# Two attention layers and two feed-forward layers on one core: the weight loads moved behind the first three quads of Q and K, and K of the second projection split on all 128 rows

## The reference, cut to what matters

```python
x = x + _L0_attn_ref(_layernorm(x), L0_attn_Wqvk, L0_attn_Wo)
x = x + _L0_ffn_ref(_layernorm(x), L0_ffn_router_w, ...)
x = x + _L1_attn_ref(_layernorm(x), L1_attn_w_q, L1_attn_w_k, ...)
x = x + _L1_ffn_ref(_layernorm(x), L1_ffn_W1, ...)
```

```python
q = q * rf
k = k * rf
qkt = jnp.einsum('brkqa,bkca->brkqc', q5, k) / scale
attn = jax.nn.softmax(qkt, axis=-1)
```

## Time and profile before

| | before |
|---|---|
| median of 3 runs | 1875.59 us (1871.88 to 1877.41) |
| profiled execution | 1856.86 us |
| its span | 1855.0 us |
| mean granted TensorE clock | 0.943 of full speed |
| TensorE matmul busy | 1708.5 us (92%) |
| TensorE weight load busy | 723.3 us (39%) |
| VectorE busy | 1372.3 us (74%) |
| ScalarE busy | 1143.6 us (62%) |
| GpSimd busy | 308.6 us (17%) |
| DMA moved | 93.73 MB, mean 51 GB/s |
| chain that ended last | PE 73%, DVE 14%, ACT 4%, issue 4%, POOL 3%, DMA 3% |

### The profile page before, as it was taken

The page is one execution under the profiler, slowest core; times in us unless marked ns, Lnnn a source line. Parts: engine busy times, 40 slices in busy tenths (PEclk is TensorE's granted clock), DMA queues, the critical chain, the costliest instruction groups (busy, mean ns, idle before and its releaser), DMA issues.

```text
span 1855.0 us, 30812 instructions
## 1 busy us (share of the span) xinstructions
PE 1708.5 (92%) x10574; PEld 723.3 (39%) x10574; DVE 1372.3 (74%) x2373; ACT 1143.6 (62%) x2396; POOL 308.6 (17%) x407
## 2 busy tenths in 40 slices
PE   6599999999999899998789999999999999999876
PEld 3244444444443366655312232232222222322455
DVE  7678888788887155464897888888888888882486
ACT  4156666756664543333406777777777777777776
POOL 5000000002231237363500000000000000000265
PEclk9589999999998899999658999999999999998998
DMA  9555454423400012222411111111111111000000
GB/s 258 137 118 127 131 141 118 49 31 56 58 22 14 26 35 71 68 67 60 119 33 14 18 18 18 18 18 18 18 18 18 18 18 18 1 2 1 1 23 24
DMA packets 97577, 93.73 MB, mean 51 GB/s; under 512 B 47214, under 2 KB 75507, under 8 KB 95376
## 3 DMA queue, kind: packets, MB, share of 16 engines
q1 hardware_dynamic: 87360, 53.70, 16.7%
q0 software_dynamic: 9920, 37.87, 5.8%
q10 hardware_dynamic: 144, 0.20, 0.1%
HBM read 48.03 MB, written 40.86 MB: 48 GB/s over the span
## 4 chain that ended last, share of the span: by engine, by line
PE 73%; DVE 14%; ACT 4%; issue 4%; POOL 3%; DMA 3%; SPq 0%; POOLq 0%; DVEq 0%; ACTq 0%
PE ps L877 20%; PE ps L861 18%; PE ps L828 17%; DVE rowmax L1513 7%; PE ps L1038 2%; PE ps L1058 2%; PE ps L1030 2%; PE ps L1048 2%; PE ps L893 2%; PE ps L831 1%; PE ps L864 1%; ACT probs L1251 1%; DMA V<-v 1%; PE ps L1015 1%; DVE K L1857 1%
## 5 line engine op out<-in xcount | busy, mean ns | idle before, releaser
L1513 DVE TENSOR_REDUCE rowmax<-ps 128x1 f32<-128x1024 f32 (+7 forms) x1024 | 977.1, 987 | 220.4 <-PE ps L828 120.9
L1251 ACT ACTIVATE probs<-ps 128x512 f32<-128x512 f32 (+3 forms) x1280 | 604.0, 537 | 268.8 <-PE ps L864 128.7
L828 PE MATMUL ps<-K,Q 72*128 72x512 bf16 (+3 forms) x1792 | 535.6, 377 | 40.2 <-DVE rowmax L1513 18.1
L861 PE MATMUL ps<-Q,K 75*128 75x512 bf16 (+3 forms) x1792 | 559.7, 364 | 11.0 <-ACT probs L1251 6.4
L861 PEld LDWEIGHTS ps<-Q,K 75*128 75x128 bf16 x1792 | 168.5, 98 | 373.4 <-ACT probs L1251 128.6
L877 PE MATMUL ps<-probs,V 128*9 128x512 f32 (+3 forms) x2560 | 289.9, 543 | 0.0
L828 PEld LDWEIGHTS ps<-K,Q 72*128 72x128 bf16 x1792 | 159.4, 99 | 280.3 <-DVE rowmax L1513 88.4
L1251 ACT ACTIVATE wu<-ps 128x512 f32<-128x512 f32 x256 | 142.0, 608 | 44.7 <-PE ps L861 43.9
L1251 ACT ACTIVATE wg<-ps 128x512 f32<-128x512 f32 x256 | 143.7, 601 | 29.0 <-PE ps L861 27.1
L616 POOL TENSOR_SCALAR rtmp<-mv 128x4 f32<-128x4 f32 x8 | 1.9, 233 | 805.6 <-DVE mv L1429 805.6
L831 PE MATMUL ps<-causal,identb 128*128 128x128 bf16 x512 | 117.0, 230 | 0.0
(11 more groups left out here) (239 smaller groups left out, 1667.8 us busy)
## 6 DMA issues: line engine op xcount, KB each, us to landing
dispatch<-wg POOLq DMA_DIRECT2D x16, 1170.0 KB, 7.9
Q<-q_parts SPq DMA_DIRECT2D x288, 64.0 KB
K<-k_parts SPq DMA_DIRECT2D x144, 64.0 KB
Q<-dispatch SPq DMA_DIRECT2D x78, 65.0 KB, 1.8
q_parts<-Q POOLq DMA_DIRECT2D x12, 384.0 KB, 4.0
probs<-returned SPq DMA_DIRECT2D x8, 512.0 KB, 3.9
V<-v SPq DMA_DIRECT2D x16, 144.0 KB
K<-k_parts SPq DMA_DIRECT2D x144, 16.0 KB
```

The lines of the kernel that those rows point to most:

```text
L828: last = pe.matmul(buf[:, c:e], Q[0:CROSS, slot, j, i * P:(i + 1) * P], K[0:CROSS, slot, kj, c:e], start=True, stop=not diag)
L861: last = pe.matmul(ps[:, bank, c:HALF], K[0:KROWS, q, kj, t * P:(t + 1) * P], Q[0:KROWS, q, j, h * HALF + c:(h + 1) * HALF], start=True, s ...
L1251: act.activation(prob(l, 4 * m + j)[:, c:HALF], ps[:, B_BANKS[(4 * m + j) % 3], c:HALF], ACT.Exp, scale=SCALE).then_inc(sl["exp_done"], 1)
L1513: dve.tensor_reduce(rowmax[:, par, 8 * j + i:8 * j + i + 1], score_a(i % 2)[:, 0:hd.keys(i)], AX, ALU.max).then_inc(sl["max_done"], 1)
```

## The change

Three things are changed. First, SP issues the twenty weight loads no longer at its start, but in layer 0 after the rows of group 0 and quad 2; quad 2 itself goes behind the rows of group 0 there. TensorE's wait for all weights moves from the start of attention 0 to the first "WO" step. Second, the K of projection 1 is computed in four chunks of 128 tokens, chunk j on the partitions 32j to 32j+31: four matmuls of 128 columns accumulate in one bank, each with a window of `wk_wide` as its weights, a tile of zeros with `wk1` in its middle. So the steps of splitting K run on 128 partitions and 128 columns. The rope factors for it are loaded in that layout (`ropeK`, four transfers by SP in the expert stage), VectorE writes `wk_wide` there too, and POOL writes K's parts with three transfers a block. Both new tiles lie in `compared`, which is free by then. Third, projection 1 uses four buffers for the parts as projection 0 does, so that the second attention's first output waits for all parts to be written. `PARTS` holds what each write adds to the ring's semaphores: 32, and 64 in projection 1.

```diff
+KVD = KV * HD
+PARTS = (32, 16 + 16 * SPL)
...
-            if l == 0 and u % 4 >= 2:
+            if u % 4 >= 2:
                 return parts_ahead[:, u % 2, :, :, :]
...
+        ropeK = compared[:, 0, 0:2 * P].rearrange("p (h n) -> p h n", h=2)
+        wk_wide = compared[:, 1, 0:2 * P - KVD]
...
-            s[l]["parts_written"] = [sem(f"parts_written{l}_{k}") for k in range((4, 2)[l])]
+            s[l]["parts_written"] = [sem(f"parts_written{l}_{k}") for k in range(4)]
...
                 sp.sem_inc(semaphore, 1)
-            for dst, source in weights:
-                sp.dma_start(dst, source).then_inc(w_in, 16)
             sp.sem_inc(ff["y_out"], FC)
...
                 sp.wait_ge(sl["v_taken"], NG + AT_ONE)
                 for written in sl["parts_written"]:
-                    sp.wait_ge(written, 32 * NG // len(sl["parts_written"]))
-                load(0, 2)
+                    sp.wait_ge(written, PARTS[l] * NG // len(sl["parts_written"]))
+                if l == 1:
+                    load(0, 2)
                 negmax_rows(0, 0)
+                if l == 0:
+                    load(0, 2)
+                    for dst, source in weights:
+                        sp.dma_start(dst, source).then_inc(w_in, 16)
...
+                            if g and t == TS:
+                                for j in range(GT):
+                                    sp.dma_start(ropeK[j * KVD:(j + 1) * KVD, :, :],
+                                                 rope[0:KVD, :].rearrange("i (h j n) -> j i h n", h=2, j=GT)[j])\
+                                        .then_inc(ropeK_in, 16)
...
-                        pool.dma_start(k_parts[l][:, :, bass.ts(u, GW)].rearrange("c p n -> p c n"),
-                                       parts_of(l, u)[0:rows_k, 1, :, :]).then_inc(written, 16)
+                        if l == 0:
+                            pool.dma_start(k_parts[l][:, :, bass.ts(u, GW)].rearrange("c p n -> p c n"),
+                                           parts_of(l, u)[:, 1, :, :]).then_inc(written, 16)
+                        else:
+                            for c in range(SPL):
+                                pool.dma_start(k_parts[l][c, :, bass.ts(u, GW)].rearrange("p (j n) -> j p n", j=GT),
+                                               parts_of(l, u)[:, 1, c, 0:P]).then_inc(written, 16)
...
-                    pe.matmul(ps[0:rk, bank + 2, :], wk, h[:, :], start=True, stop=True).then_inc(sl["k_out"], 1)
+                    if l == 0:
+                        pe.matmul(ps[:, bank + 2, :], wk, h[:, :], start=True, stop=True).then_inc(sl["k_out"], 1)
+                    else:
+                        for j in range(GT):
+                            last = pe.matmul(ps[:, bank + 2, 0:P], wk_wide[:, (GT - 1 - j) * KVD:(GT - 1 - j) * KVD + P],
+                                             h[:, j * P:(j + 1) * P], start=j == 0, stop=j == GT - 1)
+                        last.then_inc(sl["k_out"], 1)
...
                     if kind == "WO":
+                        if u == 0:
+                            pe.wait_ge(w_in, 16 * len(weights))
...
             pe.wait_ge(consts, 5)
-            pe.wait_ge(w_in, 16 * len(weights))
             attention(0)
...
-                rows = (P, P if l == 0 else KV * HD)
+                cols = (GW, GW if l == 0 else P)
...
-                            dve.tensor_tensor(qk32[0:rows[n], n, :], src[n], ropeT[0:rows[n], half * GW:(half + 1) * GW],
-                                              ALU.mult).then_inc(sl["qk_sb"], 1)
-                            src[n] = qk32[0:rows[n], n, :]
+                            dve.tensor_tensor(qk32[:, n, 0:cols[n]], src[n], angles[n], ALU.mult).then_inc(sl["qk_sb"], 1)
+                            src[n] = qk32[:, n, 0:cols[n]]
...
+                if l == 1:
+                    dve.wait_ge(ropeK_in, 16 * GT)
                 norm(0)
...
-                    if l == 0 and g == 0 and h == 0:
+                    if g == 0 and h == 0:
...
+                    if t == TS:
+                        own.done(dve.memset(wk_wide, 0.0))
+                    if t == TS + 1:
+                        apart(dve)
+                        own.done(dve.tensor_copy(wk_wide[:, (GT - 1) * KVD:GT * KVD], wk1[:, :]))
+                        dve.sem_inc(wk_placed, 1)
```

More of the change, by code:

```diff
@@ L530, in _ @@
                 for half in range(2):
-                    sp.wait_ge(sl["parts_written"][half], 32)
+                    sp.wait_ge(sl["parts_written"][half], PARTS[l])
                 for q in range(2):
@@ L1190, in body @@
                     if u >= ring:
-                        act.wait_ge(sl["parts_written"][u % ring], 32 * (u // ring))
+                        act.wait_ge(sl["parts_written"][u % ring], PARTS[l] * (u // ring))
                     for n in range(2):
-                        r = rows[n]
+                        w = cols[n]
                         if l == 0:
                             act.wait_ge(sl[("q_out", "k_out")[n]], u + 1)
-                            src = ps[0:r, 4 * half + 1 + n, :]
+                            src = ps[:, 4 * half + 1 + n, :]
                         else:
                             act.wait_ge(sl["qk_sb"], 2 * u + n + 1 + AT_ONE)
-                            src = qk32[0:r, n, :]
-                        act.activation(parts_of(l, u)[0:r, n, 0, :], src, ACT.Copy).then_inc(sl["hi_done"], 1)
+                            src = qk32[:, n, 0:w]
+                        act.activation(parts_of(l, u)[:, n, 0, 0:w], src, ACT.Copy).then_inc(sl["hi_done"], 1)
                     act.wait_ge(sl["v_out"], u + 1)
@@ L1206, in body @@
                     for n in range(2):
-                        r = rows[n]
+                        w = cols[n]
                         act.wait_ge(sl["rest_done"], 2 * u + n + 1 + AT_ONE)
-                        act.activation(parts_of(l, u)[0:r, n, 1, :], rest[0:r, n, :], ACT.Copy)\
+                        act.activation(parts_of(l, u)[:, n, 1, 0:w], rest[:, n, 0:w], ACT.Copy)\
                             .then_inc(sl["mid_done"], 1)
@@ L1468, in body @@
                 def body(u, half, more):
-                    src = [ps[0:rows[n], 4 * half + 1 + n, :] for n in range(2)]
+                    src = [ps[:, 4 * half + 1 + n, 0:cols[n]] for n in range(2)]
                     if l == 1:
+                        angles = (ropeT[:, half * GW:(half + 1) * GW], ropeK[:, half, :])
                         for n, out_sem in enumerate(("q_out", "k_out")):
@@ L1483, in body @@
                         dve.wait_ge(sl["hi_done"], 2 * u + n + 1)
-                        dve.tensor_tensor(rest[0:rows[n], n, :], src[n], parts_of(l, u)[0:rows[n], n, 0, :], ALU.subtract)\
+                        dve.tensor_tensor(rest[:, n, 0:cols[n]], src[n], parts_of(l, u)[:, n, 0, 0:cols[n]], ALU.subtract)\
                             .then_inc(sl["rest_done"], 1)
@@ L1487, in body @@
                         dve.wait_ge(sl["mid_done"], 2 * u + n + 1)
[L1488 to L1489 removed]
+                        dve.tensor_tensor(parts_of(l, u)[:, n, 2, 0:cols[n]], rest[:, n, 0:cols[n]],
+                                          parts_of(l, u)[:, n, 1, 0:cols[n]], ALU.subtract).then_inc(sl["split_done"], 1)
                 if l == 0:
                     statistics_of_batch(0)
+                if l == 1:
+                    dve.wait_ge(ropeK_in, 16 * GT)
                 norm(0)
@@ L1529, in normalise_out @@
                 def normalise_out(g, b, q, h, bank):
-                    if l == 0 and g == 0 and h == 0:
+                    if g == 0 and h == 0:
                         for written in sl["parts_written"]:
-                            dve.wait_ge(written, 32 * NG // len(sl["parts_written"]))
+                            dve.wait_ge(written, PARTS[l] * NG // len(sl["parts_written"]))
                     dve.wait_ge(sl["o_turned"], 2 * g + h + 1 + AT_ONE)
```

7 lines of the change are left out of this document (4 added, 3 removed).

## The result

The changed kernel took 1901.85 us (median of 4 runs, 1894.90 to 1903.97), the kernel before 1873.74 us beside it (4 runs, 1868.78 to 1877.41): the ratio is 1.0142, with a 95% interval of 1.0113 to 1.0171. It is 28.1 us slower on the medians and 26.6 us by the ratio; the forecast was 27.3 us. The profiled execution took 1903.82 us around a span of 1902.0, at a mean granted clock of 0.936.

The account below looks back on a forecast made before the run. TensorE bounds the first attention (busy 99.17 of 100 us), so its waits are lost. Terms -0.5 + 22.3 + 2 + 3 + 0.3 + 0.2 = +27.3 us put the time at 1903 us on the median; range 1880 to 1913.

Parts of the forecast that it names:

- Weights leave the start: Start of the kernel: taking twenty loads from ahead of the first quad gains 0.5 us, bounds nothing to 7.3.
- Quad 2 behind the first negated maxima: First attention, group 0: quad 2 issued from 92.68 us drains at 113, needed in group 2; costs nothing.
- The weights behind quad 2: SP's queue from 113.0 us: 5.72 MB at 317 GB/s take 18.0 us, ending at 131.0; bounds 16.3 to 22.
- Quad 3 and the rows behind the weights: Before group 1: quad 3 drains at 150.0, rows land at 152.5, TensorE waits 22.3 us; bounds 17.6 to 26.3.
- Fills: POOL's three dispatch-table fills start at 131 beside quad 3 and cost 2 us; bounds 0 and 9.
- (b): Rival: three fills take turns with quad 3, putting 9 us ahead of the rows instead of 2: 1910 us; chance 0.10.
- Clock: After TensorE's wait before group 1: 7 us of matmuls at half clock, 3 us net; bounds 0 and 4.
- Second projection: K in four chunks: shorter splitting steps against more POOL writes, net 0.3 us slower; bounds -7 to +4.
- Sum: All parts together: +27.3 us, 1884 on the profiled execution and 1903 on the median, 1.5% slower.
- The median as the base: The sum in microseconds was put on the three runs' median, 1875.59, not on the profiled execution's 1856.86.
- (a): Rival: weights drain beside quad 3, group 1's rows land about 3 us after 127.4; 1875 to 1868 us; chance 0.13.
- (c): Rival: weights at 350 GB/s, quad 3 at 16 us, clock not falling: +13.6 us, 1889; chance 0.10.

Follow-up runs that it names:

- Without fills: The changed kernel with POOL's first dispatch-table fills held back until the middle and end of group 1, against the kernel before: ratio 1.0115.
- small weights only: The changed kernel with the five loads of the experts' weights back at the start, the other fifteen behind quad 2, against the kernel before: ratio 1.0076.
- the weights only: The kernel before with only the weights moved behind the rows of group 0 and quad 2, its second projection unchanged: 1903.56 us, ratio 1.0177.

## Why the prediction was right

*Weights leave the start* (-0.5): ScalarE's copy for group 1 comes at 126.46 instead of 127.10, -0.6; in the other kernels it lies between 125.0 and 130.0, whether the weights are at the start or not. No gain that can be told from this spread.

*Quad 2 behind the first negated maxima* (0): nothing waits for it.

*The weights behind quad 2* (18.0 us, done at 131.0): too short by 3 to 5. POOL was released by the last weight at 135.7, in the other kernels with all twenty loads behind quad 2 and ahead of quad 3 between 133.8 and 135.1. Put as a rate from 113 us on, 5.72 MB in 22.7 us are 252 GB/s, not 317, and just beyond the upper bound of 22 us; and that although the weights did not start at 113.0, but moved 0.5 MB before. The Trainium skill, page "DMA: Bandwidth & Descriptors", section Specifications, gives the limit of about 358 GB/s that the prediction named; by it the weights would have taken 16.0 us, an estimate, and the measured time is further from that than from the forecast.

*Quad 3 and the rows behind the weights* (22.3 us): right in sum, and that was luck: two parts were off against each other. Without fills the rows landed at 151.8, against 152.5; the weights ended there at 133.9, 2.9 us later than forecast, and what quad 3 and the rows still needed behind them was 17.9 us instead of 21.5. My reading is that engines that were through with their weights early had begun with quad 3; this was not tried by itself.

*Fills* (2): some 3 (2.8 in the wait, 3.0 in the period), near the forecast and a third of rival (b)'s 9. The packets neither take turns evenly nor pass each other for nothing.

*Clock* (3): 3.2. What a period loses beyond the wait is 2.4 to 3.8 us in the kernels where TensorE waits, but 6.7 in the one with small weights only, above the bound of 4; why the clock came back so late there stays open.

*Second projection* (+0.3, bounds -7 to +4): the time alone was 1.0001. In the profiles, one of each kernel, it gained 2.0 us where the clock was at half in its last blocks both with and without the change: 926.28 to 980.22, 53.9 us, in the kernel with the weights only; 922.41 to 974.34, 51.9 us, in the changed kernel (from the first statistics to the first maximum). All eight kernels with the change lie below the two without it: 47.4 to 51.9 against 52.4 and 53.9. POOL's three writes of K did come to cost VectorE more in the early blocks, as forecast: VectorE's wait of 0.63 us for POOL becomes 2.05 in its timeline of the changed kernel:

```profile
938.88 0.87 DVE L1848 BATCH_NORM_STATS2 stats<-x 128x6 f32<-128x128 f32 x4 [2.05 <-POOLq L86]
```

POOL's timeline there has its three writes of K, 2.28 us:

```profile
931.29 2.28 POOL L708 DMA_DIRECT2D k_parts<-Q  x3
```

What the forecast got wrong is the later blocks: "nothing is shortened" there. They give back what the early blocks cost and 2 us more; which step of them does it was not tried.

*Sum*: 29.6 us in the period of group 1, less 0.6 before it and some 2 in the second projection, is 27; measured 28.1 on the medians. That the forecast's 27.3 comes within 1 us is luck in its parts: weights and quad 3 off against each other, the wait longer than forecast (26.4 against 22.3 and 2 for the fills) and the second projection shorter. The upper end of its range, 1913, does not follow from the bounds that it names: the fills at 9 and the clock at 4 give 1911.

*The median as the base.* The profiled execution of before, 1856.86, lies below all timed runs of that kernel (the fastest took 1864.78). From ScalarE's last copy of the first attention to the first statistics of the second projection it took 268.2 us, and 282.8 to 289.4 us in the nine other profiles. TensorE's busy time shows where; window 725 to 755 us of the profile of before:

```profile
725.00:755.00 30.00, 28.79 (x154) 17.99 (x153) 12.73 (x38) 10.99 (x33) 17.34 (x19) 1.00 0.22 64
```

The same window of the changed kernel:

```profile
725.00:755.00 30.00, 20.53 (x95) 13.33 (x94) 9.60 (x36) 6.30 (x20) 17.64 (x21) 0.81 0.18 49
```

So not all of the 47 us between the two profiles are the change's: 17 of them lie in this stage, and the kernel with the weights only, whose expert stage is that of before, took 287.0 us in it. Putting the sum on the median was right.

*The rivals.* (a), that the queue doesn't hold, fell with the 19.13 us in which the rows, issued, had not landed. (b) had the right direction and three times the size. (c), a short hold, fell: the weights took longer, not shorter.

## What to carry to other kernels

Loads that nobody needs soon still cost when a small, urgent transfer is issued behind them in the same queue, and the largest part of the cost may be an innocent third load that they push in front of it. Before moving bulk loads into a busy stage, list what each queue has to carry between two urgent transfers, in engine time: here a quad of 19 us in a period of 31 leaves 12, in which shares of 1.5 MB found room, but not all the weights at once. Put them behind the urgent transfer in shares, or give the urgent transfer a queue of its own, and then check the next deadline in the bulk queue.

## What the runs showed of the hardware that was not expected

An issue on SP can itself be held up: 9.26 us at a load of 1,408 KB and 14.00 us at rows of 24 KB, when much stood in the queue ahead; it blocks everything else on SP. The timeline of the kernel before has this already, at the loads of `wd` and at the first transfer of quad 1:

```profile
9.58 9.53 SPq L470 DMA_DIRECT2D wd<-in_L_ffn_down_proj_dram  x3
...
41.21 9.54 SPq L513 DMA_DIRECT2D Q<-q_parts  x1
```

The second projection and what follows it take longer or shorter with the clock they find. Its last blocks ran at 0.50 in the changed kernel and at 0.91 in the kernel with small weights only, in windows at the same place in the stage. The changed kernel:

```profile
956.00:972.00 16.00, 14.44 (x56) 11.57 (x55) 8.59 (x22) 6.41 (x16) 10.25 (x16) 0.50 0.59 147
```

The kernel with small weights only:

```profile
946.00:962.00 16.00, 11.13 (x66) 8.44 (x64) 11.23 (x30) 8.11 (x22) 12.96 (x18) 0.91 0.82 177
```

The stage took 51.9 us there and 48.0 here; the first period of the second attention's groups took 50.3 to 50.7 us in five of the ten profiles and 46.8 to 47.1 in the other five, with the same instructions. The 15 to 21 us of the expert stage that only the profile of before lacks were not expected either; between 690 and 790 us of the changed kernel VectorE stands still for 14.1 us of which the profile names no releaser, against 1.0 us in the whole stage of before. What causes them was not tried.
